# Start of a fused fc1, GELU and fc2 kernel on one core: x and fc1's first half are loaded and transposed row by row, with the first two fc1 chunks built between

## The chip, the cores and the metric

The kernel runs on one core of a Trainium2 chip. TensorE (PE) multiplies, ScalarE (ACT), VectorE (DVE) and GpSimd (POOL) do the elementwise work, SyncE (SP) and ScalarE issue the DMAs. The metric is the device time of one execution in microseconds (us). The kernel before takes 357.48 us, the median of three runs (357.47 to 357.76).

## The reference, cut to what matters

```python
# x (32, 256, 256), fc1_w (1024, 256), fc2_w (192, 1024), experts_w (16, 64, 1024)
h = gelu(einsum('bnd,hd->bnh', x, fc1_w) + fc1_b, approximate=False)
shared = einsum('bnh,sh->bns', h, fc2_w) + fc2_b
expert = einsum('bnh,bph->bnp', h, experts_w[indices]) + experts_b[indices][:, None, :]
out = x + concatenate([shared, expert], axis=-1)
```

Everything is float32. The index of a batch row picks the 64 rows of weights that make the last 64 output columns.

## The kernel before

A block is two batch rows of x (512 tokens, four tiles of 128); there are 16 blocks. Every float32 operand of a product is split in two: a high part (HI, written by ACT, which rounds it) and the remainder (LO, written by DVE or POOL), and a product is three matmuls: HI by HI, HI by LO, LO by HI. fc1 of a block is eight chunks of 128 hidden features, each by 512 tokens: `conv_chunk(c)` (line L1078) makes six matmuls of 512 columns into one PSUM bank (two halves d of the 256 input features, three matmuls each). Blocks 0 and 1 are done this way, chunks 0 to 15; blocks 2 to 15 use fewer products of 256 columns (L1110). fc2 follows chunk pairs (L1136, L1166, L1169).

The order on every engine is written out by hand and held by semaphores; nothing is scheduled by a program. What the change touches is the first 12 us:

- SP issues x's row 0 and row 1 (`resid`, 256 KB each, L318), waits for row 0 to land, then issues fc1's second half (`w_in`, 512 KB, L268), fc2's weights (`w_piece`, L323), and from there on the expert weights, x again in another layout (`pieces`) and fc1's weights in another layout (`work`, L312), with no wait before 28 us but one for the index. ACT's queue issues the index, fc1's first half (512 KB, L268) and the bias.
- PE runs 12 warm-up matmuls on an identity (`warm`, L1052, 256 columns, bfloat16), then transposes x row 0 and row 1 (`x0_banks`, L1046: four transposes each into `tr_ps`, one bank per feature half d, both rows side by side), then fc1's first half (`w1_bank(0, d)`, L1068, eight transposes into `acc_ps`), the bias (L1206), then chunk 0 (`first_chunk`, L1093, six matmuls of 512 columns with waits between), then fc1's second half (`w1_bank(1, d)`, L1068, eight transposes into `tr_ps`), then chunk 1 and the following chunks (L1086).
- ACT copies the high parts out of PSUM: `x0_high` (L461) twice, `w1_high(0, d)` (L474) twice, the GELU of chunk 0 (L577), `w1_high(1, d)` twice, the GELU of chunk 1, then fc2's weights (`w2_high`, L484). DVE writes the low parts behind it: `x0_low` (L708), `w1_low` (L721), then squares fc2's weights (`w2_square`, L744) and goes on to the expert weights and to block 1's x, whose low part (`x1_low`, L813) chunk 8 waits for. POOL makes the low part of the hidden activations (L395), and from about 30 us the sums of fc1's weights (L417).

Of the kernel before, what the change touches and what calls it, by code (L numbers as in the profile page):

```python
# [15 lines left out]
def cond_mlp_residual(nc, x, index, fc1_w, fc1_b, fc2_w, fc2_b, experts_w, experts_b, out):  # L16
# [20 lines left out]
    WARM = 12  # L37
# [29 lines left out]
    with ctx:  # L67
# [57 lines left out]
        w1_loaded = [sem(f"w1_loaded{n}") for n in range(2)]  # L125
# [141 lines left out]
        def load_w1(queue, half):  # L267
            queue.dma_start(w1_in[:, half * HALF:(half + 1) * HALF, :], w1_halves[half])\  # L268
                .then_inc(w1_loaded[half], 16)
# [4 lines left out]
        def _(sp):  # L274
# [41 lines left out]
            for b in range(R):  # L316
                ts = slice(b * T, (b + 1) * T)
                sp.dma_start(resid[:, 0, ts, :], x_blocks[0][:, ts, :]).then_inc(x0_loaded[b], 16)  # L318

            sp.wait_ge(x0_loaded[0], 16)  # L320
            load_w1(sp, 1)
# [49 lines left out]
        def _(pool):  # L371
            def residual(n, b):
                par = n % 2
                if n == 0:
                    pool.wait_ge(x0_loaded[b], 16)

                    pool.wait_ge(x0_tr, D)
# [80 lines left out]
        def _(act):  # L458
            def x0_high(d):
                act.wait_ge(x0_tr, d + 1)  # L460
                nc.scalar.activation(xt0[:, d, HI, :], tr_ps[:, d, :], ACT.Copy)\  # L461
                    .then_inc(x0_hi, 1)
# [151 lines left out]

            act.dma_start(index_sb[:, :], index.rearrange("(o n) -> o n", o=1))\
                .then_inc(index_loaded, 16)
            load_w1(act, 0)
# [8 lines left out]
            for d in range(D):  # L626
                x0_high(d)
            for d in range(D):
                w1_high(0, d)
            act.wait_ge(b1_ready, 1)  # L630
            conv_chunk(0)
            w1_high(1, 0)
            w1_high(1, 1)
# [71 lines left out]
        def _(dve):  # L705
            def x0_low(d):
                dve.wait_ge(x0_hi, d + 1)
                nc.vector.tensor_tensor(xt0[:, d, LO, :], tr_ps[:, d, :],  # L708
                                        xt0[:, d, HI, :].bitcast(FP32), ALU.subtract)\
                    .then_inc(x0_lo, 1)  # L710
# [221 lines left out]
            for d in range(D):  # L932
                x0_low(d)
            for d in range(D):
                w1_low(0, d)
            dve.wait_ge(b1_tr, 1)
# [106 lines left out]
        def _(pe):  # L1043
# [11 lines left out]
            def x0_banks(b):  # L1055
                pe.wait_ge(x0_loaded[b], 16)
                for d in range(D):
                    last = transposes(tr_ps[:, d, b * SEQ:(b + 1) * SEQ],
                                      [feature_chunk(resid[:, 0, b * T + t, :], d)
                                       for t in range(T)])  # L1060
                    if b == R - 1:
                        last.then_inc(x0_tr, 1)

            def w1_bank(half, d):

                dst = (acc_ps, tr_ps)[half][:, d, :].rearrange("p (k q c) -> p q k c", q=Q, c=S)
                for q in range(Q):
                    last = nc.tensor.transpose(  # L1068
                        dst[:, q], feature_chunk(w1_in[:, half * HALF + q, :], d), ident[:, :])
                last.then_inc(w1_tr, 1)  # L1070
# [20 lines left out]
            def first_chunk():  # L1091
                def product(d, w, v):
                    return nc.tensor.matmul(fc1_ps[:, 0, :], conv_operand(0, d, w), xt0[:, d, v, :],  # L1093
                                            start=(d == 0 and w == v), stop=(d == D - 1 and w == LO))
                for d in range(D):
                    pe.wait_ge(w1_hi, d + 1)
                    product(d, HI, HI)
                    pe.wait_ge(x0_lo, d + 1)
                    product(d, HI, LO)
                for d in range(D):  # L1100
                    pe.wait_ge(w1_lo, d + 1)
                    last = product(d, LO, HI)
                last.then_inc(conv_filled, 1)
# [96 lines left out]
            for b in range(R):  # L1200
                x0_banks(b)
            pe.wait_ge(w1_loaded[0], 16)
            for d in range(D):
                w1_bank(0, d)
            pe.wait_ge(b1_loaded, 16)
            nc.tensor.transpose(fc1_ps[:, 3, 0:K], b1_in[:, :], ident[0:K, 0:K]).then_inc(b1_tr, 1)  # L1206
            first_chunk()
            pe.wait_ge(w1_loaded[1], 16)
            for d in range(D):
                pe.wait_ge(x0_lo, d + 1)  # L1210
                w1_bank(1, d)
            conv_chunk(1)
# [105 lines left out]
```

## Time and profile before

| | |
|---|---|
| median of three runs | 357.48 us (357.47 to 357.76) |
| the profiled execution | 357.54 us |
| its span, first to last instruction | 355.4 us |
| PE busy | 350.9 us, 99% of the span |
| DVE, ACT, POOL busy | 73%, 69%, 66% |
| PE's share of the chain that ended last | 98% |

The span is what the trace covers; 2.1 us of the execution's time lie outside it. A matmul's duration in the trace is its whole flight through the array, longer than the spacing from one to the next, so the pace of a run of matmuls is the length of its piece in the chain divided by their number.

### The profile page before, as it was taken

Reading aid. Unit: us, or ns where it says so; the run is one execution under the profiler, and the core shown is the slowest. Engines: PE = TensorE matmul, PEld = TensorE weight load, DVE = VectorE, ACT = ScalarE, POOL = GpSimd, SP = SyncE. Lnnn points to the kernel's source line nnn. Section 1 sums busy time; section 2 is a strip of 40 time slices with the busy share of each in tenths; the row PEclk is TensorE's granted clock in tenths of the full one; section 3 lists DMA queues with packets and bytes.
Section 4 is the critical chain, followed back from the end, with each engine's and each line's share of the span. In section 5 each row is a group of like instructions: output and inputs, shape, how many; then the busy total and the mean of one; then the engine's idle time right before and its main releaser. Section 6 shows DMA issues by size and latency. Waiting matters only on the chain.

```text
span 355.4 us, 7075 instructions
## 1 busy us (share of the span) xinstructions
PE 350.9 (99%) x2381; PEld 323.7 (91%) x2381; DVE 259.5 (73%) x498; ACT 246.8 (69%) x410; POOL 235.0 (66%) x150
## 2 busy tenths in 40 slices
PE   8999999999999999999999999999999999999996
PEld 5899899999999999999999999999999999999996
DVE  2797976968859697786968869697786968844642
ACT  4885957777678577767777678577777777666560
POOL 0179887658866586865758866576865758855471
PEclk9999999999999999999999999999999999999999
DMA  8779663533333334341533324353332230312001
GB/s 239 172 162 191 140 181 85 148 99 89 112 87 117 89 90 141 94 110 59 149 98 89 114 79 122 90 137 101 84 107 64 90 99 30 120 38 89 31 30 61
DMA packets 69981, 37.53 MB, mean 106 GB/s; under 512 B 43450, under 2 KB 69946, under 8 KB 69946
## 3 DMA queue, kind: packets, MB, share of 16 engines
q1 hardware_dynamic: 69376, 36.55, 38.1%
q10 hardware_dynamic: 570, 0.53, 0.4%
q8 instruction: 19, 0.31, 0.4%
q14 instruction: 16, 0.13, 0.1%
HBM read 28.68 MB, written 8.39 MB: 104 GB/s over the span
## 4 chain that ended last, share of the span: by engine, by line
PE 98%; ACT 0%; issue 0%; POOL 0%; DVE 0%; POOLq 0%; ACTq 0%
PE fc_ps L1110 40%; PE acc_ps L1166 29%; PE acc_ps L1169 15%; PE fc_ps L1086 6%; PE acc_ps L1136 3%; PE acc_ps L1189 2%; PE fc_ps L1166 1%; PE fc_ps L1052 1%; PE fc_ps L1093 1%; PE fc_ps L1169 1%; PE tr_ps L1046 0%; ACT xt L461 0%; PE tr_ps L1068 0%; ACT w1t L474 0%; DVE resid L906 0%
## 5 line engine op out<-in xcount | busy, mean ns | idle before, releaser
L395 POOL TENSOR_TENSOR ht<-gelu,ht 128x1024 fp32r<-128x1024 f32 x62 | 149.5, 2411 | 97.4 <-ACT ht L565 97.4
L1166 PE MATMUL acc_ps<-w2t,ht 128*128 128x512 f32 x448 | 162.4, 397 | 0.0
L1110 PE MATMUL fc_ps<-xt,w1t 128*128 128x256 f32 x1176 | 159.9, 284 | 0.0
L1110 PEld LDWEIGHTS fc_ps<-xt,w1t 128*128 128x128 f32 x1176 | 148.7, 189 | 5.5
L1169 PE MATMUL acc_ps<-w2t,ht 128*128 128x256 f32 x448 | 125.9, 281 | 0.0
L1166 PEld LDWEIGHTS acc_ps<-w2t,ht 128*128 128x128 f32 x448 | 84.4, 188 | 14.9
L1169 PEld LDWEIGHTS acc_ps<-w2t,ht 128*128 128x128 f32 x448 | 85.0, 190 | 0.0
L565 ACT ACTIVATE ht<-gelu 128x1024 fp32r<-128x1024 f32 x64 | 68.0, 1063 | 3.6 <-issue 0.4
L591 ACT ACTIVATE gelu<-work,b 128x512 f32<-128x512 f32 x56 | 37.3, 715 | 26.2 <-DVE work L870 26.1
L403 POOL TENSOR_TENSOR xt<-work,xt 128x1024 fp32r<-128x1024 f32 x14 | 33.8, 2417 | 14.8 <-ACT xt L554 14.8
L870 DVE TENSOR_TENSOR work<-fc_ps,work 128x512 f32<-128x512 f32 x28 | 19.4, 692 | 22.6 <-PE fc_ps L1110 21.3
L863 DVE TENSOR_TENSOR work<-fc_ps,work 128x512 f32<-128x512 f32 x28 | 19.1, 681 | 20.6 <-PE fc_ps L1110 20.6
L383 POOL TENSOR_TENSOR resid<-resid,bias 128x384 f32<-128x384 f32 x32 | 33.9, 1061 | 0.0
L494 ACT ACTIVATE w2t<-tr_ps 128x512 fp32r<-128x512 f32 x28 | 16.8, 600 | 24.4 <-DVE tr_ps L763 24.4
L544 ACT ACTIVATE work<-fc_ps 128x512 f32<-128x512 f32 x28 | 16.8, 601 | 21.9 <-PE fc_ps L1110 21.8
L878 DVE TENSOR_TENSOR work<-fc_ps,work 128x512 f32<-128x512 f32 x28 | 19.4, 692 | 13.3 <-PE fc_ps L1110 13.3
L800 DVE TENSOR_TENSOR work<-b_rows 128x256 f32<-128x256 f32 x14 | 27.9, 1990 | 1.2 <-ACT b_rows L535 1.1
L930 DVE TENSOR_TENSOR resid<-acc_ps,resid 128x256 f32<-128x256 f32 x56 | 22.5, 422 | 7.3 <-PE acc_ps L1169 6.3
L603 ACT ACTIVATE gelu<-work,b 128x256 f32<-128x256 f32 x56 | 25.4, 508 | 0.0
L923 DVE TENSOR_TENSOR resid<-acc_ps,resid 128x192 f32<-128x192 f32 x56 | 19.9, 355 | 6.8 <-PE acc_ps L1169 5.8
L608 ACT ACTIVATE gelu<-fc_ps,b 128x256 f32<-128x256 f32 x56 | 23.5, 476 | 0.0
L1086 PE MATMUL fc_ps<-xt,w1t 128*128 128x512 f32 x90 | 22.0, 393 | 0.0
(73 smaller groups left out, 335.6 us busy)
## 6 DMA issues: line engine op xcount, KB each, us to landing
pieces<-in_L_cond_experts_w SPq DMA_DIRECT2D x128, 64.0 KB, 2.0
out<-resid SPq DMA_DIRECT2D x31, 256.0 KB, 3.1
pieces<-in_x SPq DMA_DIRECT2D x60, 128.0 KB, 2.9
resid<-in_x SPq DMA_DIRECT2D x15, 512.0 KB, 3.5
e_bias<-in_L_cond_experts_b SPq DMA_DIRECT2D x32, 32.0 KB, 2.8
work<-in_L_cond_fc_w SPq DMA_DIRECT2D x4, 256.0 KB, 4.7
w_piece<-in_L_cond_fc_w SPq DMA_DIRECT2D x4, 192.0 KB, 5.0
resid<-in_x SPq DMA_DIRECT2D x2, 256.0 KB, 3.2
```

The source lines that it names most:

```text
L383: nc.gpsimd.tensor_tensor(rows[:, :, 0:SHARED], rows[:, :, 0:SHARED], bias[:, :].unsqueeze(1).to_broadcast([P, T, SHARED]), ALU.add).then_ ...
L395: nc.gpsimd.tensor_tensor(ht[:, slot, LO, :, :].rearrange("p k t -> p (k t)"), gelu[:, q % GELUS, :, :].rearrange("p k t -> p (k t)"), ht[ ...
L403: nc.gpsimd.tensor_tensor(xt[:, n % 2, X_T1:X_T4 + 1, LO, :], t_sum, xt[:, n % 2, X_T1:X_T4 + 1, HI, :].bitcast(FP32), ALU.subtract).then_ ...
L565: nc.scalar.activation(ht[:, q % SLOTS, HI, :, :].rearrange("p k t -> p (k t)"), gelu[:, q % GELUS, :, :].rearrange("p k t -> p (k t)"), A ...
L591: nc.scalar.activation(gelu[:, q % GELUS, j, :], upper[:, j, :], ACT.Gelu, bias=b1[:, k:k + 1]).then_inc(up_gelu, 1)
L603: nc.scalar.activation(gelu[:, q % GELUS, j, SEQ:2 * SEQ], c22[:, j, :], ACT.Gelu, bias=b1[:, k:k + 1]).then_inc(c22_gelu, 1)
L608: nc.scalar.activation(gelu[:, q % GELUS, j, 0:SEQ], fc1_ps[:, BANK_A[t % 2], j * SEQ:(j + 1) * SEQ], ACT.Gelu, bias=b1[:, k:k + 1]).then_ ...
L800: nc.vector.tensor_tensor(t_sum[:, o, :], in0, in1, ALU.subtract)\
L1086: last = nc.tensor.matmul(fc1_ps[:, c % 4, :], conv_operand(k, d, w), xt_plain[c // K][:, d, v, :], start=(at == 0), stop=(at == len(terms ...
L1110: last = nc.tensor.matmul(fc1_ps[:, dst, j * SEQ:(j + 1) * SEQ], w1t[:, w, wv, ms], xt[:, n % 2, o, xv, :], start=(fresh and j == 0 and at ...
L1166: nc.tensor.matmul(acc.rearrange("p (v o) -> p v o", v=2), ht[:, q % SLOTS, HI, j, ts], w2t[:, :, k, fc2_columns(b)], start=(k == 0), stop ...
L1169: last = nc.tensor.matmul(acc[:, OUT:2 * OUT], ht[:, q % SLOTS, LO, j, ts], w2t[:, HI, k, fc2_columns(b)], start=False, stop=True, skip_gr ...
```

## The change

- The warm-up is 8 matmuls, not 12.
- fc1's first half is loaded as two transfers of 256 KB: two of its four strips on ACT's queue, now ahead of the index, and the other two on SP's queue between x's row 0 and row 1. SP then waits for row 0 as before.
- `tr_ps` holds one bank per row of x (both feature halves side by side) instead of one per feature half, so `x0_high` and `x0_low` work on one row at a time.
- PE transposes row 0, the two strips of the first transfer, the two of the second, then starts chunks 0 and 1 together on row 0 alone, in matmuls of 256 columns (`first`), with row 1's transposes after the first two of them. fc1's second half is transposed after row 0's twelve matmuls and ahead of row 1's twelve.
- ACT and DVE follow: row 0, fc1's first half, row 1, fc1's second half, then the GELUs of chunks 0 and 1.
- The bias is transposed after row 0's matmuls.

```diff
-    WARM = 12
+    WARM = 8
...
+        def load_w1(queue, half, part, strips):
+            cols = slice(half * HALF + strips.start, half * HALF + strips.stop)
+            queue.dma_start(w1_in[:, cols, :], w1_halves[half][:, strips])\
+                .then_inc(w1_loaded[part], 16)
+        def x0_row(v, b):
+            return xt0[:, :, v, b * SEQ:(b + 1) * SEQ]
+        def x0_bank(b):
+            return tr_ps[:, b, :].rearrange("p (d t) -> p d t", d=D)
...
                 sp.dma_start(resid[:, 0, ts, :], x_blocks[0][:, ts, :]).then_inc(x0_loaded[b], 16)
+                if b == 0:
+                    load_w1(sp, 0, 1, slice(Q // 2, Q))
             sp.wait_ge(x0_loaded[0], 16)
-            load_w1(sp, 1)
+            load_w1(sp, 1, 2, slice(0, Q))
...
+            load_w1(act, 0, 0, slice(0, Q // 2))
             act.dma_start(index_sb[:, :], index.rearrange("(o n) -> o n", o=1))\
                 .then_inc(index_loaded, 16)
-            load_w1(act, 0)
...
-            for d in range(D):
-                x0_high(d)
+            x0_high(0)
             for d in range(D):
                 w1_high(0, d)
+            x0_high(1)
+            for d in range(D):
+                w1_high(1, d)
             act.wait_ge(b1_ready, 1)
             conv_chunk(0)
-            w1_high(1, 0)
-            w1_high(1, 1)
             conv_chunk(1)
...
-            for d in range(D):
-                x0_low(d)
+            x0_low(0)
             for d in range(D):
                 w1_low(0, d)
+            x0_low(1)
...
             def x0_banks(b):
                 pe.wait_ge(x0_loaded[b], 16)
-                for d in range(D):
-                    last = transposes(tr_ps[:, d, b * SEQ:(b + 1) * SEQ], ...)
+                transposes(tr_ps[:, b, :], [feature_chunk(resid[:, 0, b * T + t, :], d)
+                                            for d in range(D) for t in range(T)]).then_inc(x0_tr, 1)
...
+            def first(c, b, d, w, v):
+                return nc.tensor.matmul(fc1_ps[:, c, b * SEQ:(b + 1) * SEQ], conv_operand(c, d, w),
+                                        xt0[:, d, v, b * SEQ:(b + 1) * SEQ],
+                                        start=(b == 0 and d == 0 and w == v), stop=True,
+                                        skip_group_check=True)
...
+            pe.wait_ge(x0_hi, 1)
+            pe.wait_ge(w1_hi, 1)
+            for c in range(2):
+                first(c, 0, 0, HI, HI)
+            x0_banks(1)
+            pe.wait_ge(w1_hi, 2)
+            for c in range(2):
+                first(c, 0, 1, HI, HI)
+            pe.wait_ge(x0_lo, 1)
+            for d in range(D):
+                for c in range(2):
+                    first(c, 0, d, HI, LO)
+            for d in range(D):
+                pe.wait_ge(w1_lo, d + 1)
+                for c in range(2):
+                    first(c, 0, d, LO, HI)
...
+            pe.wait_ge(x0_lo, 2)
+            pe.wait_ge(w1_loaded[2], 16)
             for d in range(D):
-                pe.wait_ge(x0_lo, d + 1)
-                w1_bank(1, d)
-            conv_chunk(1)
+                w1_strips(1, d, range(Q)).then_inc(w1_tr, 1)
+            for c in range(2):
+                for d in range(D):
+                    for w, v in ((HI, HI), (HI, LO), (LO, HI)):
+                        last = first(c, 1, d, w, v)
+                last.then_inc(conv_filled, 1)
             conv_chunk(2)
```

PE's program from the warm-up to chunk 2, of the kernel before (`w_in` is fc1's weights as loaded, `tr_ps` and `acc_ps` where they are transposed to, `fc_ps` the chunks' banks):

```order
L1052 MATMUL fc_ps<-ident 128x256 [waits ident_ready]
L1052 MATMUL fc_ps<-ident 128x256 x11
...
L1046 MATMUL tr_ps<-ident,resid 128x128 [waits x0_loaded1]
...
L1068 MATMUL acc_ps<-ident,w_in 128x4x32 [waits w1_loaded0]
L1068 MATMUL acc_ps<-ident,w_in 128x4x32 x7
L1206 MATMUL fc_ps<-ident,b_in 128x8 [waits b1_loaded]
L1093 MATMUL fc_ps<-xt,w1t 128x512 [waits w1_hi]
L1093 MATMUL fc_ps<-xt,w1t 128x512 [waits x0_lo]
...
L1093 MATMUL fc_ps<-xt,w1t 128x512 [waits w1_lo] x2
L1068 MATMUL tr_ps<-ident,w_in 128x4x32 [waits x0_lo,w1_loaded1]
...
L1086 MATMUL fc_ps<-xt,w1t 128x512 x12
```

The same stretch of the changed kernel (its own line numbers):

```order
L1059 MATMUL fc_ps<-ident 128x256 x7
L1053 MATMUL tr_ps<-ident,resid 128x128 [waits x0_loaded0]
...
L1071 MATMUL acc_ps<-ident,w_in 128x4x32 [waits w1_loaded0]
...
L1071 MATMUL acc_ps<-ident,w_in 128x4x32 [waits w1_loaded1]
...
L1096 MATMUL fc_ps<-xt,w1t 128x256 [waits w1_hi,x0_hi]
...
L1053 MATMUL tr_ps<-ident,resid 128x128 [waits x0_loaded1]
...
L1096 MATMUL fc_ps<-xt,w1t 128x256 [waits w1_hi]
...
L1096 MATMUL fc_ps<-xt,w1t 128x256 [waits x0_lo]
...
L1221 MATMUL fc_ps<-ident,b_in 128x8 [waits b1_loaded]
L1071 MATMUL tr_ps<-ident,w_in 128x4x32 [waits w1_loaded2,x0_lo]
...
L1096 MATMUL fc_ps<-xt,w1t 128x256 x12
L1089 MATMUL fc_ps<-xt,w1t 128x512 x6
```

Row 1's transposes stand behind the first two products, and the transposes of fc1's second half stand ahead of half of chunks 0 and 1 instead of between the two chunks.

ACT's program after the index and table loads, of the kernel before:

```order
L461 ACTIVATE xt<-tr_ps 128x512 [waits x0_tr,gelu_loaded]
L461 ACTIVATE xt<-tr_ps 128x512 [waits x0_tr]
L474 ACTIVATE w1t<-acc_ps 128x2x256 [waits w1_tr] x2
L577 ACTIVATE gelu<-fc_ps,b 128x512 [waits conv_filled,b1_ready]
L474 ACTIVATE w1t<-tr_ps 128x2x256 [waits w1_tr] x2
L577 ACTIVATE gelu<-fc_ps,b 128x512 [waits conv_filled]
L484 ACTIVATE w2t<-acc_ps 128x2x192 [waits w2_sq] x2
```

And of the changed kernel:

```order
L470 ACTIVATE xt<-tr_ps 128x2x256 [waits x0_tr,gelu_loaded]
L482 ACTIVATE w1t<-acc_ps 128x2x256 [waits w1_tr] x2
L470 ACTIVATE xt<-tr_ps 128x2x256 [waits x0_tr]
L482 ACTIVATE w1t<-tr_ps 128x2x256 [waits w1_tr] x2
L585 ACTIVATE gelu<-fc_ps,b 128x512 [waits conv_filled,b1_ready]
L585 ACTIVATE gelu<-fc_ps,b 128x512 [waits conv_filled]
L492 ACTIVATE w2t<-acc_ps 128x2x192 [waits w2_sq] x2
```

Row 1's copy stands behind fc1's first half, and the two GELUs stand together, right ahead of fc2's weights.

## Rows read from the trace of the kernel before

**Rows 1.** The page, part 1: busy time, share of the span, instructions.
```profile
PE 350.9 (99%) x2381; PEld 323.7 (91%) x2381; DVE 259.5 (73%) x498; ACT 246.8 (69%) x410; POOL 235.0 (66%) x150
```

**Rows 2.** Waits, 20 to 355 us: PE's only two (waited for, us, times, longest).
```profile
PEld acc_ps L1189 <- POOL ht L395: 0.3, 1, 0.3
PEld fc_ps L1166 <- POOL ht L395: 0.2, 1, 0.2
```

**Rows 3.** Chain that ended last, 0 to 24 us: start us, us, what.
```profile
1.53 2.74 PE fc_ps L1052 x12
4.28 1.13 PE tr_ps L1046 x6
...
7.19 1.46 PE fc_ps L1093 x5
...
9.17 0.95 PE tr_ps L1068 x8
10.11 9.57 PE fc_ps L1086 x42
19.68 2.87 PE acc_ps L1136 x24
```

**Rows 4.** Line L1052, then L1046 early and late: ns min/median/max, first and last start.
```profile
L1052 PE MATMUL fc_ps<-ident x12: 395/421/422, 1.5 to 3.9; 128*128 128x256 bf16 x12
L1046 PE MATMUL tr_ps<-ident,resid x3: 364/421/421, 4.1 to 4.5; 128*128 128x128 f32 x3
L1046 PE MATMUL tr_ps<-ident,resid x6: 273/284/386, 4.5 to 5.3; 128*128 128x128 f32 x6
```

**Rows 5.** Timeline, 0 to 30 us: start, us, instructions [idle before, releaser].
```profile
3.51 0.37 SPq L268 DMA_DIRECT2D w_in<-in_L_cond_fc_w  x1
...
4.88 0.55 PEld L1046 LDWEIGHTS tr_ps<-ident,resid 128*128 128x128 f32 x4 [0.16 <-DMA resid<-in_x]
5.49 1.09 ACT L461 ACTIVATE xt<-tr_ps 128x512 fp32r<-128x512 f32 x2 [1.74 <-PE tr_ps L1046]
5.75 1.03 PEld L1068 LDWEIGHTS acc_ps<-ident,w_in 128*128 128x128 f32 x8 [0.32 <-DMA w_in<-in_L_cond_fc_w]
```

**Rows 6.** DMA by stretch: us, busy (x) of PE, PEld, DVE, ACT, POOL, PEclk, DMA share, GB/s.
```profile
1.75:2.50 0.75, 0.75 (x5) 0.56 (x4) 0.00 (x0) 0.24 (x1) 0.00 (x0) 1.00 0.56 157
2.50:5.00 2.50, 2.50 (x14) 1.91 (x13) 0.00 (x0) 1.24 (x2) 0.00 (x0) 1.00 1.04 356
```

**Rows 7.** Line L268, fc1's two transfers: time from issue to landing.
```profile
DMA to landing us min/median/max: 4.0/4.2/4.4
```

**Rows 8.** Line L323, fc2's weights: issues, and time from issue to landing.
```profile
L323 SPq DMA_DIRECT2D w_piece<-in_L_cond_fc_w x4: 441/444/511, 3.9 to 5.4; - x4
...
DMA to landing us min/median/max: 4.5/5.0/5.6
```

**Rows 9.** Timeline again, where ACT and DVE take over fc1's second half and fc2's weights.
```profile
10.47 1.29 DVE L721 TENSOR_TENSOR w1t<-tr_ps,w1t 128x512 fp32r<-128x512 f32 x2 [1.80 <-ACT w1t L474]
...
11.54 0.69 ACT L577 ACTIVATE gelu<-fc_ps,b 128x512 f32<-128x512 f32 x1 [0.61 <-PE fc_ps L1086]
11.68 1.04 DVE L744 STREAM_TRANSPOSE acc_ps<-w_piece 128x384 f32<-128x384 f32 x2
12.30 0.95 ACT L484 ACTIVATE w2t<-acc_ps 128x384 fp32r<-128x384 f32 x2
...
19.52 3.04 PE L1136 MATMUL acc_ps<-w2t,ht 128*128 128x256 f32 x24
...
20.73 1.29 DVE L813 TENSOR_TENSOR xt<-tr_ps,xt 128x512 fp32r<-128x512 f32 x2 [0.43 <-ACT xt L515]
...
22.39 1.55 PE L1086 MATMUL fc_ps<-xt,w1t 128*128 128x512 f32 x6
```

**Rows 10.** POOL's timeline, 28 to 44 us.
```profile
28.37 2.40 POOL L403 TENSOR_TENSOR xt<-work,xt 128x1024 fp32r<-128x1024 f32 x1
30.74 2.01 POOL L417 TENSOR_TENSOR w_in<-work 128x512 f32<-128x512 f32 x1
```

More of the change, by code:

```diff
@@ L124, in cond_mlp_residual @@
         stored = [sem(f"stored{n}") for n in range(2)]
-        w1_loaded = [sem(f"w1_loaded{n}") for n in range(2)]
+        w1_loaded = [sem(f"w1_loaded{n}") for n in range(3)]
         w1p_loaded = sem("w1p_loaded")
@@ L265, in bank @@
             return fc1_ps[:, i, :].rearrange("p (j t) -> p j t", j=2)
-        def load_w1(queue, half):
-            queue.dma_start(w1_in[:, half * HALF:(half + 1) * HALF, :], w1_halves[half])\
-                .then_inc(w1_loaded[half], 16)
+        def load_w1(queue, half, part, strips):
[6 more added lines that the diff above has]
+            return tr_ps[:, b, :].rearrange("p (d t) -> p d t", d=D)
         block = ctx.enter_context(nc.Block())
@@ L375, in residual @@
                     pool.wait_ge(x0_loaded[b], 16)
-                    pool.wait_ge(x0_tr, D)
+                    pool.wait_ge(x0_tr, R)
                 else:
@@ L458, in _, with x0_high @@
         def _(act):
[L459 to L462, printed above, removed]
+            def x0_high(b):
+                act.wait_ge(x0_tr, b + 1)
+                nc.scalar.activation(x0_row(HI, b), x0_bank(b), ACT.Copy).then_inc(x0_hi, 1)
             def w1_slots(half, d, v):
@@ L705, in _, with x0_low @@
         def _(dve):
[L706 to L710, printed above, removed]
+            def x0_low(b):
+                dve.wait_ge(x0_hi, b + 1)
+                nc.vector.tensor_tensor(x0_row(LO, b), x0_bank(b), x0_row(HI, b).bitcast(FP32),
+                                        ALU.subtract).then_inc(x0_lo, 1)
             def w1_slots(half, d, v):
@@ L1056, in x0_banks, with w1_strips @@
                 pe.wait_ge(x0_loaded[b], 16)
-                for d in range(D):
[L1058 to L1064, printed above, removed]
+                transposes(tr_ps[:, b, :], [feature_chunk(resid[:, 0, b * T + t, :], d)
+                                            for d in range(D) for t in range(T)]).then_inc(x0_tr, 1)
+            def w1_strips(half, d, strips):
                 dst = (acc_ps, tr_ps)[half][:, d, :].rearrange("p (k q c) -> p q k c", q=Q, c=S)
-                for q in range(Q):
+                for q in strips:
                     last = nc.tensor.transpose(
                         dst[:, q], feature_chunk(w1_in[:, half * HALF + q, :], d), ident[:, :])
-                last.then_inc(w1_tr, 1)
+                return last
             def conv_operand(j, d, v):
@@ L1089, in conv_chunk @@
                 last.then_inc(conv_filled, 1)
[L1091 to L1097, printed above, removed]
-                    pe.wait_ge(x0_lo, d + 1)
[L1099 to L1103, printed above, removed]
+            def first(c, b, d, w, v):
[3 more added lines that the diff above has]
+                                        skip_group_check=True)
             def product(n, g, dst, w, o, fresh):
@@ L1199, in _ @@
             warm(WARM)
-            for b in range(R):
-                x0_banks(b)
+            x0_banks(0)
             pe.wait_ge(w1_loaded[0], 16)
             for d in range(D):
-                w1_bank(0, d)
+                w1_strips(0, d, range(Q // 2))
+            pe.wait_ge(w1_loaded[1], 16)
+            for d in range(D):
+                w1_strips(0, d, range(Q // 2, Q)).then_inc(w1_tr, 1)
+            pe.wait_ge(x0_hi, 1)
[14 more added lines that the diff above has]
+                    first(c, 0, d, LO, HI)
             pe.wait_ge(b1_loaded, 16)
             nc.tensor.transpose(fc1_ps[:, 3, 0:K], b1_in[:, :], ident[0:K, 0:K]).then_inc(b1_tr, 1)
-            first_chunk()
-            pe.wait_ge(w1_loaded[1], 16)
+            pe.wait_ge(x0_lo, 2)
+            pe.wait_ge(w1_loaded[2], 16)
             for d in range(D):
-                pe.wait_ge(x0_lo, d + 1)
-                w1_bank(1, d)
-            conv_chunk(1)
+                w1_strips(1, d, range(Q)).then_inc(w1_tr, 1)
+            for c in range(2):
+                for d in range(D):
+                    for w, v in ((HI, HI), (HI, LO), (LO, HI)):
+                        last = first(c, 1, d, w, v)
+                last.then_inc(conv_filled, 1)
             conv_chunk(2)
```

## The prediction

> **What bounds the kernel now.** Read the page's busy shares first: PE is busy 99% of the span, the other engines 66 to 73% [rows 1]. Then the waits from 20 us on: PE waited there twice in 335 us, 0.5 us in all, both near the end for POOL [rows 2]. So from the first full chunk on PE never stands still, and a change in the first 12 us is worth what it moves the beginning of that unbroken run, unless something else is then late. Then the chain over the first 24 us [rows 3]: warm-up, transposes, a hop to ACT, chunk 0, transposes, and from 9.9 us a solid run of matmuls. Three paces come out of it: 512 columns take 9.57 / 42 = 0.228 us each, 256 columns 2.87 / 24 = 0.12, a 128 x 128 transpose 0.95 / 8 = 0.12.
>
> The warm-up does not run at that pace: its 12 matmuls of 256 columns start from 1.5 to 3.9 us, 2.32 / 11 = 0.21 us apart, and fly 421 ns [rows 4]. x's early transposes fly 421 ns, the last of them 284 [rows 4]. That is TensorE's clock at its lower level (1.2 GHz) until about 4.7 us and at the upper one (2.4 GHz) after it, though the granted clock column reads 1.00 throughout [rows 6]. Before it rose PE had worked without a gap from 1.53 us.
>
> The beginning is read against one mark, the start of chunk 2, which both kernels reach with the same work behind it. Before: fc2 starts at 19.52 [rows 9], and chunks 2 to 7 are 36 matmuls ahead of it, 36 x 0.228 = 8.2, so 11.3 us.
>
> **The change part by part, as a timetable up to that mark.**
>
> *Warm-up, 8 for 12.* It now ends at 1.53 + 8 x 0.21 = 3.2 instead of 4.07. x row 0 has landed at 3.5, for SP's transfer that waits for it goes at 3.51 [rows 5]; PE then stood in the warm-up for another half microsecond. That is what the edit sets free.
>
> *First transfers.* Row 0 now shares the DMA engines with 256 KB of fc1 from the start, where ACT's transfer stood behind the index before. From below row 0 lands as before, 3.5: from 1.75 to 2.5 us the engines were busy 0.56 of the time and had room [rows 6]. From above it waits for all of the other 256 KB at 356 GB/s [rows 6], 0.74 later, 4.25. I take 3.65, near the lower end, as the idle share speaks for. The second pair of strips stands where row 1 stood on SP's queue, which landed at 4.88 at the latest [rows 5]; row 1 is now the last of the same 1 MB that was in by 5.75 [rows 5]. fc1's second half is issued 0.15 later, 3.66, and lands 4.0 to 4.4 after that [rows 7], by 8.1; it is wanted at 8.6.
>
> The Trainium skill's DMA: Bandwidth & Descriptors (Queues, rings and completion order) says that each DMA engine takes its queues in turn, a packet at a time. By that alone row 0 would wait for nearly all of the other 256 KB, the 4.25 of the upper end; no row separates the queues, so the trace neither bears it out nor speaks against it.
>
> *PE to the first product.* Row 0's four transposes start at 3.7, 0.21 apart, the last at 4.33, landing 0.42 later at 4.75. Then the two strips of the first transfer: four transposes, 4.55 and 4.75, 4.87, 4.99 as the clock rises where it did; the other two strips from 5.11, which is past their landing. The high part of fc1 for d = 0 needs two of these: 5.23 + 0.28 = 5.5. ACT has done row 0 by then (from 4.85, 0.6 long), takes fc1 from 5.55 to 6.15, and PE's first product starts at 6.2. Before it was 7.19 [rows 3]: 1.0 earlier.
>
> *PE from the first product to chunk 2.* This is longer than before. Two products (restart after a wait 0.1, 2 x 0.12) end the slot at 6.55; row 1's four transposes, formerly ahead of everything, take until 7.0, and the last lands at 7.2. Behind them ten products of row 0 at 0.12 and the bias at 0.2, all of whose operands are ready, end at 8.4. The next instruction, fc1's second half into `tr_ps`, waits for DVE to have read row 1 out of it: ACT 7.3 to 7.9 (0.6 for 512 columns [rows 5]), DVE 7.93 to 8.6 (0.69 [rows 9]), so PE stands 0.2 and goes on at 8.65. Queued behind that wait is all of PE's program. Then restart 0.1, eight transposes 0.96, row 1's twelve products 1.44: chunk 2 at 11.15. Before, the same stretch from 7.19 to 11.3 took 4.1; now 4.95, because four transposes moved in (0.5), 24 matmuls of 256 columns cost 24 x 0.12 = 2.88 for 12 x 0.228 = 2.74 (0.14), the bias came in (0.2), and the waits are about as long as before. The restart and a mix of kinds may cost 0.1 more or less.
>
> *Sum.* 11.15 - 11.3 = -0.15 to -0.2. I take -0.17. The profiled execution took 357.54 (span 355.4 and 2.1 around it), so 357.37; the median is 0.06 lower, so 357.3.
>
> *What is late next.* Chunk 8 starts at 22.39 and needs DVE's low part of block 1's x, done at 20.73 + 1.29 = 22.02 [rows 9]: 0.37 of room. Does DVE's chain come earlier too? Its `w1_low` of the second half moves from 10.47 to 10.15, so fc2's first square from 11.68 to 11.36, past its last transfer (landed by 5.4 + 5.6 = 11.0 [rows 8], plus 0.15). But ACT has both GELUs ahead of fc2's high part now: chunk 0's ends its flight at 10.8, GELU 10.85 to 11.54, the second 11.57 to 12.26, and `w2_high` cannot start before 12.2; it started at 12.30 [rows 9]. So DVE's chain, which alternates with ACT from there, stays where it was, and whatever PE gains over 0.37 it gives back at chunk 8. The same limit stands once more: POOL's sums of fc1's weights start at 30.74, right behind work that ends at 30.77 [rows 10], and their transfer is in SP's queue without regard to PE, so a gain of the compute can't move them much.
>
> *The rest* (one bank per row instead of per d, the index behind a transfer, POOL's wait on the same transposes) costs nothing: same sizes, and the index is first read at 7 us.
>
> **The rivals.**
>
> *A, slower: the clock rises later.* Where PE before worked from 1.53 to the rise without a gap, it now stands from 3.2 to 3.7. For: that gap is the only new thing before the rise. Against: it is 0.45 in 3.1 us. Place and price: if it stays low until row 1 is transposed, fc1's transposes for d = 0 are complete at 5.56 + 0.42 = 6.0 instead of 5.5; the first product and row 1's transposes run at 0.21, from 6.65 to 7.95, the last landing at 8.15 instead of 7.2; ACT and DVE bring PE on at 9.6; chunk 2 at 9.6 + 2.5 = 12.1, which is 0.8 later than before; 0.5 if ACT's and the restart's gaps close up. It decides from about 0.3 of delay at row 1's last transpose on. Time 358.0 to 358.3.
>
> The Trainium skill's TensorE: Matmul & The Clock Gate (Part 1: The HAM clock gate) says that the half clock is the default, that sustained activity lifts it, and that the point differs from run to run. By that rule a thinner start may lift it later; this trace shows one rise only and cannot say.
>
> *B: row 0 lands at the upper end, 4.25.* Then PE idles a whole microsecond behind the warm-up, everything to chunk 2 moves by 0.3 to 0.5, since part of it is hidden in ACT's hop, and SP, which waits for row 0, issues each later transfer 0.75 later. fc1's weights for POOL, used with no room at 30.77 [rows 10], are then late as well. -0.17 + 0.3 to 0.7: 357.5 to 358.0.
>
> *C: all of the earlier start comes through.* If row 1's round trip is short enough, PE gains more, up to the 1.0 of the first product. Chunk 8 stops it at 0.37: 357.1. Beyond that ACT's and DVE's chain would have to come earlier too, and only then could it be 356.7.
>
> *D: the halves don't land one after the other*, the second pair coming with the first or later than 5.1. Before 5.1 it costs nothing, and at 5.4 it moves the first product by 0.3: 357.5.
>
> **How the numbers follow.** The forecast (row 0 by 3.8, clock as before) 0.58, with its own range 357.1 to 357.5; A 0.18; B and D 0.17; C up to the limit 0.04, beyond it 0.03. The forecast, B, D, C leave 357.0 to 357.9, and A's middle is 358.1; the range 357.0 to 358.1 leaves out half of A and C's far end, about 0.15. What a measurement of this kernel can tell from no change is 0.2%, 0.7 us: faster means under 356.8, which only C's far end and an unforeseen gain reach, 0.05; slower means over 358.2, which is A's upper half and B together with A, 0.13; the rest, 0.82, is no change.
>
> **What would show it.** In the changed trace: warm-up ending at 3.2 and row 0's transposes at 3.5 to 3.8; their flight of 421 ns ending near 4.7, else A; the first product at 6.2; a PE wait of 0.2 for DVE's low part of row 1 ending at 8.65; chunk 2 at 11.15; `w2_high` at 12.2 to 12.3 and `x1_low` ending at 22.0; no PE wait between 12 and 340 us. The forecast is wrong if the first product is not about 1.0 earlier, if the stretch from it to chunk 2 isn't about 0.85 longer, or if PE waits at chunk 8 or after.

## The result, and the profile after

| | before | changed |
|---|---|---|
| median, first comparison | 357.48 us (357.28 to 357.82) | 358.81 us (357.74 to 359.08) |
| ratio to before, 95% interval | | 1.0026 (1.0018 to 1.0035) |
| the same kernel on another chip | 357.70 us | 359.07 us, 1.0036 (1.0023 to 1.0049) |
| profiled execution | 357.54 us, span 355.4 | 358.23 us, span 356.1 |

The changed kernel is slower by 0.3%, where 357.3 us and no change were forecast. Its runs also lie 1.3 us apart, where those of before lie 0.5 apart. (The ratio on record is not the quotient of the medians, which would be 1.0037.)

The page of the changed kernel, part 1, and its waits of PE from 12 us on (waited for, us, times, longest), the counterparts of [rows 1, 2]:

```profile
PE 350.7 (98%) x2389; PEld 324.1 (91%) x2389; DVE 259.7 (73%) x498; ACT 247.0 (69%) x410; POOL 235.1 (66%) x150
```

```profile
PEld acc_ps L1185 <- POOL ht L404: 0.3, 1, 0.3
PEld fc_ps L1162 <- POOL ht L404: 0.2, 1, 0.2
```

From 12 us on PE waits twice, for POOL, as before, 0.5 us in all. The loss is in the first 12 us. The chain that ended last, 0 to 24 us, of the changed kernel (start us, us, what), against [rows 3]:

```profile
0.75 3.40 DMA resid<-in_x
...
4.20 1.13 PE tr_ps L1053 x4
5.32 1.29 PE acc_ps L1071 x6
...
6.64 0.61 ACT w1t L482
7.25 0.14 issue
7.38 0.47 PE fc_ps L1096 x2
7.85 0.50 PE tr_ps L1053 x4
...
8.38 0.61 ACT xt L470
...
9.01 0.70 DVE xt L716
...
9.76 1.23 PE tr_ps L1071 x8
10.98 1.43 PE fc_ps L1096 x12
12.41 8.19 PE fc_ps L1089 x36
20.60 2.87 PE acc_ps L1132 x24
```

It begins with row 0's transfer, landing at 4.15 (before: 3.5 [rows 5]). Six of fc1's transposes then take 1.29, 0.21 each: the lower clock. fc2, in the middle of PE's long run, starts 0.92 later than before (20.60 against 19.68 [rows 3]). The rest, from there to the end, is 0.13 shorter than before (where, no row here shows), and the span is 0.8 longer.

The flight times (lines L1053, L1071 and L1096, starts in the last column) say where the clock was:

```profile
L1053 PE MATMUL tr_ps<-ident,resid x4: 418/418/487, 4.2 to 4.9; 128*128 128x128 f32 x4
L1071 PE MATMUL acc_ps<-ident,w_in x4: 418/418/418, 6.0 to 6.6; 128*128 128x128 f32 x4
L1096 PE MATMUL fc_ps<-xt,w1t x2: 282/319/356, 7.4 to 7.6; 128*128 128x256 f32 x2
```

The matmul at 6.6 still flies at the lower level (1.2 GHz), the products from 7.4 on at the upper (2.4 GHz); before, the clock rose at about 4.7 [rows 4]. DMA by stretch, as in [rows 6]:

```profile
1.75:2.50 0.75, 0.75 (x5) 0.56 (x4) 0.00 (x0) 0.30 (x1) 0.00 (x0) 1.00 0.54 120
2.50:4.25 1.75, 0.98 (x6) 0.37 (x4) 0.00 (x0) 1.19 (x2) 0.00 (x0) 1.00 1.06 344
5.25:6.00 0.75, 0.75 (x6) 0.75 (x5) 0.00 (x0) 0.58 (x1) 0.00 (x0) 1.00 0.44 40
```

The idle share before 2.5 us was not filled by the second transfer: 0.54 against 0.56, and no more bytes. The view by queue says why. From 1.75 to 2.5 us only SP's queue (q1) moved anything, though ACT had sent its part at 0.74. From 2.5 to 3.5 us the two shared the engines (packets, MB, share of 16 engines; the changed kernel, then before, where ACT's queue, q10, had hardly begun):

```profile
q1 hardware_dynamic: 169, 0.17, 57.3%
q10 hardware_dynamic: 145, 0.15, 45.4%
```

```profile
q1 hardware_dynamic: 318, 0.31, 90.1%
q10 hardware_dynamic: 18, 0.02, 8.5%
```

So row 0 had about half of the engines for the rest of its way. From 5.25 to 6 the engines run nearly dry: SP sent the next transfer only at 4.17.

The changed kernel was run once more for a second trace. Expected before it ran: PE's gap leaves it to chance when the clock rises, so the low flights end at another moment than in the first trace and the time follows; the rival was a rise at the same moment and a time within 0.2 us. The rival failed. With row 0 landing as before, the chain that ended last shows what the spread is made of:

```profile
4.20 1.12 PE tr_ps L1053 x4
5.33 1.29 PE acc_ps L1071 x6
...
7.38 0.77 PE fc_ps L1096 x2
8.15 0.85 PE tr_ps L1053 x4
9.01 1.50 PE fc_ps L1096 x10
10.50 0.15 PE fc_ps L1221
10.66 1.15 PE tr_ps L1071 x8
11.81 1.43 PE fc_ps L1096 x12
13.24 8.19 PE fc_ps L1089 x36
```

The first product starts at 7.38 in both, but here row 1's four transposes take 0.85 instead of 0.50, since the clock stays low until about 9.4, and the long run starts at 13.24 instead of 12.41. That execution took 359.07 us, the other 358.23: 0.83 in the start, 0.84 in the time.

### The profile page after: what moved, and what is told of

Read it like the earlier page. It is cut to its first block, busy times and chain, and to the rows that moved or that the text cites. A ratio compares the mean times of both kernels' runs of the same rounds, so it can differ in the third digit from the quotient of the medians.

```text
span 356.1 us, 7093 instructions
## 1 busy us (share of the span) xinstructions
PE 350.7 (98%) x2389; PEld 324.1 (91%) x2389; DVE 259.7 (73%) x498; ACT 247.0 (69%) x410; POOL 235.1 (66%) x150
## 4 chain that ended last, share of the span: by engine, by line
PE 97%; DMA 1%; ACT 0%; DVE 0%; issue 0%
PE fc_ps L1106 40%; PE acc_ps L1162 29%; PE acc_ps L1165 15%; PE fc_ps L1089 5%; PE acc_ps L1132 3%; PE acc_ps L1185 2%; PE fc_ps L1162 1%; DMA resid<-in_x 1%; PE fc_ps L1096 1%; PE fc_ps L1165 1%; PE tr_ps L1053 0%; PE acc_ps L1071 0%; PE tr_ps L1071 0%; DVE xt L716 0%; ACT xt L470 0%; ACT w1t L482 0%
## 5 line engine op out<-in xcount | busy, mean ns | idle before, releaser
L1089 PE MATMUL fc_ps<-xt,w1t 128*128 128x512 f32 x84 | 20.6, 391 | 0.0
```

What stands on the lines that cost most here:

```text
L1089: last = nc.tensor.matmul(fc1_ps[:, c % 4, :], conv_operand(k, d, w), xt_plain[c // K][:, d, v, :], start=(at == 0), stop=(at == len(terms ...
```

## The experiments

Fifteen runs were made in four groups, two of them of before and of the changed kernel once more. Each group ran on one chip with runs of before beside it, whose medians were 357.71 us (warm8_alone, transfers_alone, changed_warm12, index_first_warm12), 357.70 (changed_again, changed_warm12_nowait, row1_first, warm10_alone), 357.62 (before_again, warm8_again, order_alone, parts_on_sp) and 357.39 (the other three). All have the full computation. Times in the traces are us from the span's start; "low until / high from" are the starts of the last matmul with the low flight and the first with the high one, so where PE stands the rise can lie anywhere between the two. (The first transpose after a stand flies longer than the next ones at either level: up to 389 ns with 283 behind it, 485 to 489 with 417 to 421.)

| kernel | row 0 landed | low until / high from | first product | chunk 2 | traced execution | median (range) | ratio (95%) |
|---|---|---|---|---|---|---|---|
| before | 3.49 | 4.28 / 4.69 | 7.19 | 11.33 | 357.54 | 357.48 (357.28-357.82) | |
| before_again | 3.55 | 6.48 / 6.91 | 7.76 | 11.75 | 357.92 | 357.46 (357.33-357.92) | 0.9994 (0.9985-1.0003) |
| warm10_alone | 3.69 | 4.23 / 5.18 | 7.51 | 11.62 | 357.67 | 357.66 (357.29-359.09) | 1.0004 (0.9993-1.0015) |
| warm8_alone | 3.72 | 8.61 / 9.44 | 8.01 | 12.46 | 358.42 | 358.67 (357.81-359.58) | 1.0027 (1.0014-1.0040) |
| warm8_again | 3.75 | 5.01 / 5.40 | 7.44 | 11.43 | 357.48 | 357.48 (357.21-358.72) | 0.9996 (0.9983-1.0010) |
| transfers_alone | 3.99 | 4.53 / 5.84 | 8.08 | 12.30 | 358.24 | 358.51 (358.24-359.44) | 1.0025 (1.0008-1.0042) |
| order_alone | 3.60 | 10.00 / 10.41 | 8.15 | 13.86 | 360.02 | 359.79 (358.62-360.05) | 1.0051 (1.0037-1.0065) |
| order_alone_again | 3.60 | 4.71 / 5.89 | 7.65 | 12.53 | 358.33 | 359.92 (358.33-360.82) | 1.0078 (1.0064-1.0091) |
| order_alone_filled | 3.59 | 6.36 / 6.92 | 7.97 | 12.84 | 358.68 | 358.57 (358.40-359.02) | 1.0033 (1.0021-1.0045) |
| changed | 4.15 | 6.61 / 7.38 | 7.38 | 12.25 | 358.23 | 358.81 (357.74-359.08) | 1.0026 (1.0018-1.0035) |
| changed_again | 4.15 | 9.23 / 9.63 | 7.38 | 13.08 | 359.07 | 359.07 (358.16-359.48) | 1.0036 (1.0023-1.0049) |
| changed_warm12 | 3.99 | 4.75 / 5.14 | 6.67 | 11.71 | 358.11 | 358.16 (357.38-359.13) | 1.0014 (1.0005-1.0022) |
| changed_warm12_nowait | 4.05 | 5.23 / 5.64 | 6.94 | 11.88 | 357.87 | 358.23 (357.87-359.84) | 1.0022 (1.0011-1.0033) |
| row1_first | 4.02 | 4.07 / 4.32 | 6.84 | 11.38 | 357.56 | 358.33 (357.56-359.97) | 1.0019 (1.0008-1.0030) |
| row1_first_filled | 4.34 | 6.16 / 6.59 | 7.64 | 11.95 | 357.77 | 358.39 (357.77-360.43) | 1.0032 (1.0018-1.0045) |
| index_first_warm12 | 3.48 | 5.53 / 5.96 | 7.24 | 12.12 | 358.25 | 358.69 (358.08-359.07) | 1.0027 (1.0016-1.0039) |
| parts_on_sp | 3.66 | 4.28 / 4.66 | 7.48 | 11.92 | 357.93 | 358.25 (357.66-360.98) | 1.0026 (1.0010-1.0042) |

The start of chunk 2 carries the time: from there to the end of the span the seventeen traces differ by no more than 0.6 us (343.7 to 344.3), while chunk 2 itself starts between 11.33 and 13.86.

**The warm-up alone.** The kernel before with `WARM = 8` (warm8_alone, and warm8_again on another chip), and with `WARM = 10`:

```diff
-    WARM = 12
+    WARM = 8
```

> The kernel before with 8 warm-up matmuls, nothing else. Theory (the clock rises later because PE stands before it): row 0 lands at 3.5 as before, so PE stands only 0.3 us from 3.2 to 3.5; if that short gap is enough, the flight of 421 ns lasts beyond 6.6 as in the changed kernel and the time is 0.4 to 0.9 us above before; if it isn't, the clock rises near 4.7, and the time is that of before within 0.1, because PE waits for row 1 at 4.88 either way. Rival (the clock has no part in it, the landings and the order do all of it): 0.0 in either case.

Line L1068 of warm8_alone, then of warm8_again (flight ns min/median/max, first and last start; `acc_ps` is fc1's first half, `tr_ps` the second):

```profile
L1068 PE MATMUL acc_ps<-ident,w_in x8: 421/421/487, 5.9 to 7.5; 128*128 128x128 f32 x8
L1068 PE MATMUL tr_ps<-ident,w_in x8: 273/283/283, 10.1 to 11.0; 128*128 128x128 f32 x8
```

```profile
L1068 PE MATMUL acc_ps<-ident,w_in x8: 281/283/387, 6.0 to 6.9; 128*128 128x128 f32 x8
L1068 PE MATMUL tr_ps<-ident,w_in x8: 271/283/283, 9.1 to 9.9; 128*128 128x128 f32 x8
```

PE stood 0.56 us before row 0 in both (0.3 was expected; row 0 landed 0.2 later). The first trace has the lower clock in fc1's transposes and in half of chunk 0, until about 9.4, and chunk 2 1.1 later than before; the second is as before.

> The kernel before with 8 warm-up matmuls, a second trace. Theory (with the gap before row 0 the rise is left to chance): a gap of 0.3 to 0.6 us again, and a rise at another moment than 9.4, with the time following it: if it rises near 5 the time is that of before, if at 9 about 1 us more; over the runs +0.9 us and a spread over 1 us. Rival (the gap always costs one fixed delay): the rise at 9.4 again within 0.3.

The rise was elsewhere, so there is no fixed delay; but on this chip the median is that of before, where +0.9 was expected, and only three of eleven runs were above 358.2 (358.27, 358.57 and 358.72). The same gap cost 1.0 us in the median on one chip and nothing on the other; whether that is the chip or chance is not shown.

> The kernel before with 10 warm-up matmuls, nothing else; they end at 3.65, when row 0 has just landed, so PE has no gap there. Theory (it is the gap before row 0 that delays the clock, and 8 warm-up matmuls alone leave one of 0.5 us): the clock rises near 4.7 to 5 and the time is that of before within 0.15 us. Rival (it is the number of warm-up matmuls): the clock rises after 6 and the time is 0.4 us or more above before.

Here the warm-up ended as row 0 landed. The median is that of before, so the number 12 as such is not needed; two of its twelve runs took 358.94 and 359.09.

**The changed kernel with its warm-up of 12.**

```diff
-    WARM = 8
+    WARM = 12
```

> The changed kernel with 12 warm-up matmuls instead of 8. Theory (of the loss against before most is the clock, which rose late since PE stood from 3.2 to 4.2): the warm-up reaches to 4.1, PE has no gap, the clock rises near 4.7, first product at 6.4, chunk 2 at 11.35, time equal to before within 0.15 us, so about 1.0 less than the changed kernel, and its spread back from 1.3 us to about 0.5. Rival (the late landing of row 0 and the longer stretch from the first product to chunk 2 cost it, the clock nothing): chunk 2 at 12.2 as in the changed kernel, +0.9 us.

Half right: in its trace PE has no gap, the clock rises near 5, the first product is at 6.67, 0.7 earlier than in the changed kernel (of which 0.16 is row 0). Chunk 2 is at 11.71 instead of 11.35, and the time 0.45 above before. Its waits of PE and of PE's weight loads from 8 us on, and the step of its chain with the transfer, give the rest:

```profile
PE tr_ps L1071 <- DMA w_in<-in_L_cond_fc_w: 0.3, 1, 0.3
```

```profile
PEld acc_ps L1132 <- POOL ht L404: 0.4, 1, 0.4
```

```profile
4.01 5.11 DMA w_in<-in_L_cond_fc_w
```

fc1's second half, sent at 4.01, lands 5.1 later, at 9.12, and fc2's weights at 12.57; so ACT's and DVE's chain is late, POOL behind it, and fc2 waits 0.4 at its start, which no earlier trace had. The transfers and their order are those of the changed kernel, where the same transfer landed at 8.03 and 8.36, so these alone don't make it late; nor is it the pace as a whole, for by 8 us the engines had moved 1.80 MB here and 1.79 in the changed kernel.

**The transfers alone**, in the order of work of before:

```diff
+                if b == 0:
+                    load_w1(sp, 0, 1, slice(Q // 2, Q))
...
+            load_w1(act, 0, 0, slice(0, Q // 2))
             act.dma_start(index_sb[:, :], ...)
-            load_w1(act, 0)
...
+            pe.wait_ge(w1_loaded[1], 16)
```

> The kernel before, 12 warm-up matmuls and its order of work, with the new transfers only (first half of fc1 in two, ACT's part ahead of the index, the other between row 0 and row 1). Theory (row 0 shares the engines with ACT's part and lands at 4.15): row 0 lands at 4.1 to 4.2, just as the warm-up ends at 4.1, so PE hardly stands and the clock rises near 4.7; row 1 lands at 5.9, fc1's first half by 5.3, so the first product comes 0.4 to 0.5 later than before; time +0.4 us. Rival (row 0 was late in one execution by chance): row 0 at 3.5 to 3.7 and +0.2 us for row 1 alone.

Row 0 at 3.99 and the clock as expected, but 0.8 us instead of 0.4: row 1 lands at 5.80 (before 4.84), and in this order ACT can't copy either bank without it, so the first product comes 0.9 later.

**The order alone**, twice, and with its gaps filled:

```diff
-                if b == 0:
-                    load_w1(sp, 0, 1, slice(Q // 2, Q))
...
-            load_w1(act, 0, 0, slice(0, Q // 2))
...
+            load_w1(act, 0, 0, slice(0, Q))    # behind the index
...
-            pe.wait_ge(w1_loaded[1], 16)
...
-    WARM = 8
+    WARM = 12
```

> The changed kernel's order of work with the transfers of before and 12 warm-up matmuls. Theory (the new order pays only if fc1's first half is there by 5, and its stretch from the first product to chunk 2 is 0.8 longer): fc1's first half lands at 5.7 to 6.0, first product at 7.3 to 7.5, chunk 2 at 12.1 to 12.3, time +0.7 to +0.9 us over before, without any delay of the clock (low flights end by 5.3). Rival (the order costs nothing, since row 1's trip is hidden): first product 7.3, chunk 2 at 11.4, time as before.

Slower than either expected: +2.2 us. The timeline of PE (start, us, instructions, idle before):

```profile
4.07 1.06 PE L1051 MATMUL tr_ps<-ident,resid 128*128 128x128 f32 x4
5.82 1.98 PE L1069 MATMUL acc_ps<-ident,w_in 128*128 128x128 f32 x8 [0.70 <-DMA w_in<-in_L_cond_fc_w]
8.15 0.77 PE L1094 MATMUL fc_ps<-xt,w1t 128*128 128x256 f32 x2 [0.35 <-ACT w1t L480]
8.72 1.05 PE L1051 MATMUL tr_ps<-ident,resid 128*128 128x128 f32 x4
9.43 1.86 PE L1094 MATMUL fc_ps<-xt,w1t 128*128 128x256 f32 x10
```

Here the warm-up has no gap behind it; PE stands for fc1's first half (0.70) and for ACT, and the clock stays low until 10.0. It was open whether such gaps are the cause or the chip is; the next two ran on one chip.

```diff
             x0_banks(0)
+            warm(4)
             pe.wait_ge(w1_loaded[0], 16)
...
+            warm(3)
             pe.wait_ge(x0_hi, 1)
```

> The new order with the transfers of before and 12 warm-up matmuls, once more, as the partner of the next kernel on the same chip. Theory (PE's gaps at 5.0 to 5.8 and ahead of the first product let the clock's rise slip): rise after 6.5, chunk 2 at 12.5 to 13.9, time +1.2 to +2.2 us. Rival (the late rise was that chip's): rise before 5.5, chunk 2 at 12.2, time +0.8 us.

> The same kernel with 4 warm-up matmuls between row 0's transposes and fc1's, and 3 between fc1's and the first product, where PE stood before; they fit in the gaps. Theory (the gaps cause the late rise): low flights end by 5.3 to 7, chunk 2 at 12.1 to 12.4, time +0.7 to +1.0 us over before, that is 0.5 us or more less than its partner, and a spread under 0.8 us. Rival (chance or the chip alone): the same time and the same spread as its partner.

The filled kernel's PE timeline:

```profile
4.07 1.06 PE L1051 MATMUL tr_ps<-ident,resid 128*128 128x128 f32 x4
4.92 1.06 PE L1057 MATMUL fc_ps<-ident 128*128 128x256 bf16 x4
5.87 1.57 PE L1069 MATMUL acc_ps<-ident,w_in 128*128 128x128 f32 x8
7.27 0.49 PE L1057 MATMUL fc_ps<-ident 128*128 128x256 bf16 x3
7.98 0.47 PE L1094 MATMUL fc_ps<-xt,w1t 128*128 128x256 f32 x2 [0.21 <-ACT w1t L480]
```

Seven more matmuls whose result nobody reads make the median 1.35 us lower (358.57 in six runs against 359.92 in five), and the spread falls from 2.5 us to 0.6; order_alone, the same kernel as the unfilled one, had 359.79 on its chip. This is the strongest sign that the gaps in PE's work ahead of the rise make a late clock likelier. It is not shown in the traces of this pair: the trace of the unfilled kernel happened to be its fastest run (358.33, clock high by 5.89), its others lie around 360, and the filled one rose later (6.4 to 6.9). The slow kind is seen in order_alone's trace alone (360.02, low until 10.0). What is left at +1.2 us is the order with a late first half (first product 7.65 to 7.97) and a rise at 6.4 to 6.9 even so.

**Where row 0 and the later transfers land.** The index back ahead of ACT's part, against changed_warm12:

```diff
-            load_w1(act, 0, 0, slice(0, Q // 2))
             act.dma_start(index_sb[:, :], ...)
+            load_w1(act, 0, 0, slice(0, Q // 2))
```

> The changed kernel with 12 warm-up matmuls and with the index back ahead of ACT's part of fc1, as its transfers were ordered before. Theory (row 0 was late because ACT's part started at the same time): ACT's data starts after 3 us again, row 0 lands at 3.5; the warm-up ends at 4.07, fc1's parts land by 4.5 and 4.9, first product at 6.15, chunk 2 at 11.15, time 0.1 to 0.2 us below before. Rival (any splitting of fc1's first half delays row 0, wherever the index is): row 0 at 4.1 again and the time as with 12 warm-up matmuls alone.

Row 0 landed at 3.48, as the theory says: it is ACT's part beside it that makes it late. But that part then landed at 5.21 and the first product came at 7.24; nothing was won (358.69, 1.0 us above the 357.71 of before on that chip). SP's wait taken away:

```diff
-            sp.wait_ge(x0_loaded[0], 16)
             load_w1(sp, 1, 2, slice(0, Q))
```

> The changed kernel with 12 warm-up matmuls and without SP's wait for row 0 ahead of fc1's second half. Theory (what remained of the loss at 12 warm-up matmuls comes from SP: it sends fc1's second half only when row 0 has landed, the engines run dry from 5.3 to 6, and fc1's second half and fc2's weights land at 9.1 and 12.6 instead of 7.5 and 11.1): fc1's second half lands by 7.6 and fc2's weights by 11.3, PE waits neither for them nor for POOL at fc2's start, time 0.5 us less than with 12 warm-up matmuls alone, that is within 0.15 us of before. Rival (the stretch from the first product to chunk 2 is what costs it): the landings come earlier, and the time stays at +0.4 us or more.

Wrong. The transfer was sent at 2.26 instead of 4.01 and still landed at 9.28, fc2's weights at 12.32; the time stayed. SP's wait is not what makes them late here. On top of it, row 1 before the first product:

```diff
+            x0_banks(1)
             pe.wait_ge(x0_hi, 1)
             pe.wait_ge(w1_hi, 1)
             for c in range(2):
                 first(c, 0, 0, HI, HI)
-            x0_banks(1)
```

> As the kernel above (12 warm-up matmuls, no wait on SP), and row 1 is transposed before the first product instead of behind the first two. Theory (row 1's round trip over ACT and DVE is what PE waits for before fc1's second half): row 1 lands at 5.8 while PE stands for fc1's high part anyway, so its low part is ready at 8.6, PE goes on to fc1's second half at 8.6 instead of 9.2, chunk 2 at 11.1 to 11.2, time 0.1 to 0.3 us below before, no more since chunk 8 waits for DVE. Rival (ACT and DVE are the bound of that stretch, not PE's order): chunk 2 as without this edit, time equal to it.

The trace is the best of the kernels with the new order: low until 4.07, chunk 2 at 11.38 (11.1 to 11.2 was expected), 357.56 us. Its clock rose 1.3 earlier than in the kernel that it is compared with, so what the place of row 1 is worth is not shown. The chain shows what holds it there:

```profile
2.26 6.52 DMA w_in<-in_L_cond_fc_w
8.78 0.14 issue
8.92 1.19 PE tr_ps L1070 x8
10.11 1.43 PE fc_ps L1095 x12
```

fc1's second half, landed at 8.78. The median is still 0.6 above the 357.70 of before on that chip, where -0.1 to -0.3 was expected. The same with four warm-up matmuls more, behind fc1's first transposes and ahead of row 1's:

```diff
+            warm(4)
             x0_banks(1)
```

> The version with 12 warm-up matmuls, no wait on SP and row 1 transposed before the first product, with 4 warm-up matmuls in the gap before row 1's transposes. Theory: PE works without a gap over 0.4 us until about 6.8, the clock rises by 5.5 in most runs, chunk 2 near 11.4, median within 0.2 us of before instead of +0.6. Rival (its +0.6 comes from the late landings of fc1's second half and fc2's weights): median as without the filling, +0.5 us or more.

Not so: 358.39, 1.0 above before, and as wide. Here filling won nothing. Its row 0 landed at 4.34, so PE stood 0.3 behind the warm-up, and its clock rose after 6.2; the rival's late landings (8.83 and 12.08) stand in the trace too. This run doesn't separate the two. The last one is row1_first with both parts on SP's queue behind row 0, none on ACT's, and SP's wait back:

```diff
                 if b == 0:
+                    load_w1(sp, 0, 0, slice(0, Q // 2))
                     load_w1(sp, 0, 1, slice(Q // 2, Q))
+            sp.wait_ge(x0_loaded[0], 16)
...
-            load_w1(act, 0, 0, slice(0, Q // 2))
```

> The changed kernel with 12 warm-up matmuls, row 1 transposed before the first product, and both parts of fc1's first half on SP's queue between row 0 and row 1, none on ACT's. Theory (row 0 is late because it shares the engines with ACT's part): row 0 lands at 3.5 to 3.7 again, the two parts at 4.3 to 4.6 and 5.0 to 5.3, row 1 by 6.0; first product at 6.3; PE then waits for fc1's second half, issued at 3.6 and landing at 8.5 to 9, so chunk 2 at 11.0 to 11.5 and the time within 0.2 us of before. Rival (splitting itself, more transfers in flight, makes row 0 late): row 0 at 4.0 or later, first product at 6.8.

Row 0 at 3.66, as expected, but the second part at 6.15 and row 1 at 6.88, each about a microsecond later than worked out: from 3.5 to 5 us the engines moved 242 GB/s here against 380 in changed_warm12. With one queue the pace was lower; whether the single queue is the reason was not tested. First product 7.48, +0.6 us.

**The control.**

> The kernel before once more, for a second trace of it. Theory (PE without a gap from 1.5 us on gets the clock by about 5): low flights end by 5.3, first product at 7.2 to 7.5, chunk 2 at 11.3 to 11.6, time equal to before. Rival (the moment is a matter of chance for this kernel too): low flights past 6 and chunk 2 at 12 or later, in this trace.

The rival is right on the moment: in this execution of before, without a gap before row 0, some of fc1's transposes still fly low, the last at 6.48:

```profile
L1068 PE MATMUL acc_ps<-ident,w_in x8: 273/328/444, 6.0 to 7.3; 128*128 128x128 f32 x8
```

PE stood only once before that, for 0.2 us at 4.9, for row 1. It cost this execution 0.4 (357.92, its slowest run), and the eleven runs are within 0.6 us. Of the 94 runs of before beside the four groups three were above 358.3 (358.56, 359.55 and 359.63), so before has late starts too, but rarely. That it has less to lose, since its chunk 0 is six matmuls between waits for ACT and DVE and not twelve products and four transposes in a row, is argued and not tested.

## Why the prediction was wrong, step by step

- *Warm-up.* Ended at 3.2 as worked out. The half microsecond set free was not there to win.
- *First transfers.* The first step that failed: "I take 3.65, near the lower end, as the idle share speaks for". Row 0 landed at 4.15, near the upper end of 4.25 that the text had worked out (rival B, 0.17 together with D). It landed at 3.5 to 3.75 in every trace in which ACT's data starts at 2.8 us or later, or ACT sends no part of fc1, and at 4.0 to 4.35 where it starts at 2.5 to 2.6. The idle share was time in which only SP's transfer had started; after it the two queues shared the engines, 0.17 and 0.15 MB in a microsecond. The text says that no row separates the queues; the view by queue of the trace of before would have. This is +0.5 at row 0.
- *The clock.* The second, and the heavier: "as the clock rises where it did" (rival A, 0.18). Row 0's lateness doubled the gap that A spoke of, from 0.45 to 0.98. In the first trace six transposes at 0.21 brought the first product to 7.38 instead of 6.2: 0.5 from row 0, 0.7 from the clock; in the second the products too ran slow, 0.8 more. The text names "B together with A" only for a time over 358.2 and gives it no timetable; they came together, and the late landing lengthened the gap. A's price, chunk 2 at 12.1 and so 0.95 behind the forecast, lies between the 0.7 that the clock cost in the first trace and the 1.5 in the second. That the low flights cost this is shown; that the gap is why the clock was late is likely and not proved (below).
- *First product to chunk 2.* Right: 4.95 worked out, 7.38 to 12.25 = 4.87 measured, where before has 4.1. So the new order pays only if its first product comes over 0.7 earlier than before's; it came 0.2 later. With the warm-up back at 12 it came at 6.67, 0.5 earlier, and the kernel was at +0.14%.
- *Late next.* Chunk 8 did not wait: `x1_low` ended at 22.74 (22.0 was forecast) and chunk 8 started at 23.31. fc1's second half landed at 8.03, by 8.1 as forecast; fc2's weights landed at 11.62, 0.5 later than worked out, and `w2_high` started at 13.04 instead of 12.2 to 12.3. In the other kernels with the split transfers fc1's second half landed at 8.6 to 9.3, up to 1.8 later than before's 7.51, which cost up to 0.4 at fc2's start.
- *The range* ended at 358.1, below A's own upper end of 358.3 and with no room for A and B together.

Left open: why the clock rose late in one run and not in the next of the same kernel; why fc1's second half lands near 9 in most kernels with the split transfers, even when it is sent 1.8 us earlier, and near 8 in the changed one; why 8 warm-up matmuls alone cost 1.0 on one chip and nothing on another; and what the 0.6 us of row1_first is made of in the runs that have no trace.

## What to carry to other kernels

Let a warm-up reach to the landing of what it waits for: in the kernel before 12 and 10 matmuls did and gave 357.5 and 357.7, 8 did not and gave 358.7 on one chip and 357.5 on the other. A later gap before the clock has risen is worth trying to fill with matmuls that nobody reads: in one of two trials seven of them lowered the median by 1.35 us, in the other four did nothing. A second transfer issued beside the one that the start waits for takes its share of the engines, even where the profile shows them half idle at first; look at the traffic by queue. When two rivals share a cause, price them together: here the late landing lengthened the gap ahead of the clock's rise.

## What the runs showed of the hardware that was not expected

The rise of the clock, in seventeen traces of nearly the same start, lies between 4.1 and 10.4 us, with the first matmul always at 1.53. It is not tied to the number of warm-up matmuls. In the nine traces in which PE stood nowhere longer than 0.2 us before the rise, it came by 6.9; of the eight with a longer stand (0.3 to 1.0 us) four had it at 6.6 to 10.4 and four between 4.7 and 6.6. The three latest, past 8.6 us, all have one of half a microsecond or more; so a gap goes with a late rise, but doesn't always bring one. The view's granted clock reads 1.00 for all of these stretches; the flight times show the lower level (417 to 421 ns against 283 for the same transpose).

The Trainium skill's TensorE: Matmul & The Clock Gate (Part 1: The HAM clock gate) says that the half clock is the default and that the moment of the rise differs from run to run. These runs agree, and the same kernel traced twice had it about 2 us apart (before, before_again) and 3 to 6 us apart (warm8_alone, warm8_again; order_alone, order_alone_again), more than that page's half a microsecond.
